# Score attention phase of a gated cross-attention stack: TensorE's order in half 1, the query banks, and two groups of warm-up matmuls

## The reference, cut to what matters

```python
# L1 feed-forward: dense base product plus a sparsely gated low-rank product
logits = sigmoid(xf @ router_W.T)                       # 32 values, each repeated twice
logits = repeat(logits, 2) + biases
top_v, top_i = top_k(logits, 8)
gating = sparse / sum(sparse) * 8
out = xf @ base_W.T + 2.0 * ((xf @ A.T) * gating) @ B.T
# L2 "score" attention: queries and keys come from the context, the layernorm of x
# multiplies the scores elementwise, and the softmax itself is the block's output
scores = (ctx @ Wq.T + bq) @ (ctx @ Wk.T + bk).T / 8 * layernorm(x)
x = x + tanh(g) * softmax(where(mask, -inf, scores))
# L2 experts: their router
logits = layernorm(x) @ router_w.T                      # 8 experts, top 2, capacity 64
```

## Time and profile before

| | |
|---|---|
| median of three runs | 1154.47 us (1151.9 to 1156.37) |
| the profiled execution's own time | 1155.46 us |
| its span, first to last instruction | 1153.7 us |
| mean granted TensorE clock | 0.939 of full speed |
| TensorE busy | 1016.7 us, 88% of the span |
| VectorE, ScalarE, GpSimd busy | 708.8, 483.2, 195.4 us |

### The profile page before, as it was taken

One profiled execution on the slowest core, in us unless ns is written; L12 is line 12 of the kernel. 1 busy time (PEld: TensorE's weight loads), 2 busy tenths in 40 slices (PEclk: granted clock), 3 DMA queues, 4 the chain that ended last, 5 costly groups with the idle time before them and its releaser, 6 DMA issues. The chain is left out here.

```text
span 1153.7 us, 23269 instructions
## 1 busy us (share of the span) xinstructions
PE 1016.7 (88%) x9296; PEld 830.5 (72%) x9296; DVE 708.8 (61%) x1737; ACT 483.2 (42%) x863; POOL 195.4 (17%) x167
## 2 busy tenths in 40 slices
PE   7979889769998899999789999885796989889997
PEld 4747777658777687878678887674694777677886
DVE  0667768766776665564576666666535677654544
ACT  1447767613343335444233333334442334333443
POOL 4100000020001133444430000032101000133342
PEclk8999999988999899999899999986797999888999
DMA  8600000000001122333000000010100000122232
GB/s 291 226 2 3 2 1 2 2 1 1 2 3 34 52 94 77 99 96 97 8 1 2 2 2 2 1 38 1 37 1 1 2 3 18 33 96 80 87 106 69
DMA packets 17707, 48.29 MB, mean 42 GB/s; under 512 B 3072, under 2 KB 5248, under 8 KB 17472
## 3 DMA queue, kind: packets, MB, share of 16 engines
q1 hardware_dynamic: 17600, 46.80, 12.5%
HBM read 45.61 MB, written 1.05 MB: 40 GB/s over the span
## 5 line engine op out<-in xcount | busy, mean ns | idle before, releaser
L1567 POOL TENSOR_TENSOR p_WML<-p_raw,p_WMH 128x768 fp32r<-128x768 f32 x56 | 103.5, 1849 | 173.8 <-ACT p_WMH L1652 168.3
L1683 ACT ACTIVATE p_AHI<-p_A 128x512 fp32r<-128x512 f32 x62 | 39.2, 632 | 168.5 <-DVE p_A L1765 168.5
L1765 DVE TENSOR_TENSOR p_A<-p_A,PS 128x512 f32<-128x512 f32 x62 | 42.6, 688 | 85.0 <-PE PS L1615 84.4
L1288 ACT ACTIVATE p_E<-PS 128x768 f32<-128x768 f32 x64 | 51.6, 807 | 83.3 <-PE PS L1139 83.3
L1393 DVE TENSOR_REDUCE p_mx<-PS 128x2 f32<-128x512 f32 x64 | 44.1, 689 | 59.2 <-PE PS L1103 59.1
L737 PE MATMUL PS<-p_FT,p_PTS 128*128 128x128 f32 x512 | 65.2, 281 | 16.1 <-DVE XNS L889 14.8
L737 PEld LDWEIGHTS PS<-p_FT,p_PTS 128*128 128x128 f32 x512 | 61.2, 195 | 22.0 <-DVE p_PTS L925 20.7
L1769 DVE TENSOR_TENSOR p_ALO<-p_A,p_AHI 128x512 fp32r<-128x512 f32 x62 | 44.8, 723 | 43.2 <-ACT p_AHI L1683 43.2
L83 PE MATMUL PS<-p_WMH,p_AHI 128*128 128x256 f32 x224 | 63.1, 282 | 3.5 <-DVE p_ALO L1769 3.3
L85 PE MATMUL PS<-p_WMH,p_ALO 128*128 128x256 f32 x224 | 62.5, 279 | 0.0
L84 PE MATMUL PS<-p_WML,p_AHI 128*128 128x256 f32 x224 | 62.5, 279 | 0.0
(11 more groups left out here) (504 smaller groups left out, 3290.7 us busy)
## 6 DMA issues: line engine op xcount, KB each, us to landing
p_raw<-in_moe SPq DMA_DIRECT2D x56, 448.0 KB, 3.3
p_fr<-in_fold SPq DMA_DIRECT2D x16, 480.0 KB, 4.5
p_raw<-in_wpack SPq DMA_DIRECT2D x8, 416.0 KB, 6.2
p_early_raw<-in_moe SPq DMA_DIRECT2D x6, 448.0 KB, 3.2
CP<-in_consts SPq DMA_DIRECT2D x1, 1725.0 KB, 9.9
XS<-in_x SPq DMA_DIRECT2D x1, 1024.0 KB, 14.9
W2R<-in_ffn SPq DMA_DIRECT2D x4, 256.0 KB, 3.6
p_W3R<-in_ffn SPq DMA_DIRECT2D x4, 256.0 KB
```

What stands on the lines that cost most here:

```text
L1288: act.activation(E[:, n % 4], PS[:, ST:ST + 2, 0:384], ACT.Exp, scale=scale).then_inc(s["ex"], 1)
L1567: g.tensor_tensor(WML[:, n % RING, :], raw[:, i % RAW, 0:SEL], WMH[:, n % RING, 0:SEL].bitcast(F32), ALU.subtract).then_inc(s["w_lo"], 1)
L1765: v.tensor_tensor(A[:, b, :], A[:, b, :], PS[:, GS_BANK, :], ALU.mult).then_inc(s["ag"], 1)
```

## The change

TensorE's list is changed in one place: `base(1)` moves from behind `query_keys(1)` to directly behind `mid_router(1)`, ahead of `lora(0)`; `lora_turned(1)` moves ahead of the wait for both evictions and asks for one of them only; the queries and keys of half 1 go to banks 3 and 7 in place of 0 and 1. Two groups of eight warm-up matmuls are added, one behind `transposes(0)` and one behind `transposes(1)`. The lists of the other engines stay as they are.

```diff
--- before.py
+++ after.py
@@ -2182,7 +2182,7 @@
                 CNT = ph.sb("CNT", [P, NT, 2 * NE])
                 junk = ph.sb("junk", [P, 1])
 
-                QP, TR, BASE, MR, MT, SC = (((7, 3), (0, 1)), (0, 0), (4, 0), (2, 6), (7, 3), (6, 2))
+                QP, TR, BASE, MR, MT, SC = (((7, 3), (3, 7)), (0, 0), (4, 0), (2, 6), (7, 3), (6, 2))
 
                 with nc.Block() as block:
                     @block.sync
@@ -2241,7 +2241,7 @@
                         def lora_turned(h):
                             for t in range(TT):
                                 pe.wait_ge(s[h]["ga"], t + 1)
-                                pe.wait_ge(s[0]["q_raw"], 2)
+                                pe.wait_ge(s[h]["q_raw"], 2 if h == 0 else 1)
                                 m = pe.transpose(PS[0:LR, MT[h], t * P:t * P + P], M[h][:, t, :], ident)
                             m.then_inc(s[h]["mt"], 1)
 
@@ -2277,11 +2277,12 @@
                         lora_turned(0)
                         pe.wait_ge(s[1]["t1_lo"], KC)
                         mid_router(1)
+                        base(1)
                         lora(0)
+                        pe.wait_ge(s[0]["q_raw"], 2)
                         query_keys(1)
+                        lora_turned(1)
                         pe.wait_ge(s[1]["q_raw"], 2)
-                        base(1)
-                        lora_turned(1)
                         scores(0)
                         lora(1)
                         scores(1)
@@ -2289,7 +2290,9 @@
                         pe.wait_ge(s[1]["es"], 2)
                         warm(pe, WARM["mid"], bank=BASE[0])
                         transposes(0, s[0]["n3"], s[0]["t3_done"], BASE[0])
+                        warm(pe, WARM["split"], bank=3)
                         transposes(1, s[1]["n3"], s[1]["t3_done"], BASE[1], s[1]["n3d"])
+                        warm(pe, WARM["split"], bank=3)
                         for h in range(HALVES):
                             logits(h)
                         for h in range(HALVES):
```

## The result

The changed kernel took 1159.36 us in the median of eight runs (1156.88 to 1161.44), the kernel before 1154.43 us in eight of its own (1151.9 to 1156.64). The ratio is 1.0036, 95% interval 1.0018 to 1.0053: about 4 us slower. The profiled execution took 1157.01 us, only 1.55 above the profiled one of before; its phases ahead of the changed one, whose code is the same, happened to be 1.8 us shorter.

A forecast was written before the change was run, and what follows sets the result against it. No engine fills the phase; a chain passing from engine to engine bounds it. 1155.46 + 2.7 - 1.0 = 1157.2 us for an execution like the profiled one, 0.99 above the median, so forecast 1156.2 us; range 1152.6 to 1159.6.

The forecast's parts named there:

- rival (b): Second warm-ups ahead of the logits warm nothing, logits stay at 0.213 us each: +4.5, 1159.0 us; chance 0.08.
- The queue on GpSimd: Queries 1 finish late behind base(1), delaying GpSimd's list, its statistics and half 0's normalisation and scores: +2.7 us.
- Its lower bound: In the front, the clock rises one stretch earlier, base(1) ends at 766.9, and the cost is only 1.1 us.
- TensorE's removed wait: TensorE's 0.78 us of waiting for the eviction of queries goes; nobody profits.
- VectorE's wait for the turned middle: VectorE's 2.80 us wait at 773.77, which lora_turned(1) causes, ends in slack; VectorE gains nothing there.
- First warm-ups: Eight behind transposes(0), 1.8 us at full clock, fit the 2.33 us idle ahead of transposes(1): zero cost.
- Second: Warm-ups ahead of the logits cost 1.8 us but speed the logits to 0.104 us each: net gain 1.0 us.
- The rule on weight loads: At the logits, a 128-column weight load takes 107 ns whatever the clock, so a higher clock would gain nothing.
- that moment moves against the rise of the clock: The next phase's start shifts against the clock's rise: put at zero, with 0.7 us either way.
- (a): Clock up earlier or unseen slack in the chain: +1.1 in front, -1.4 behind, 1154.2 us; chance 0.22.
- (d): Another wait hides the front, only the tail counts, next phase starts near a rise: -2.1, 1152.4 us; chance 0.08.
- (c): Clock stays at 1.2 GHz through the changed phase because of added idle time: +9.8, 1164.3 us; chance 0.05.

The follow-up runs named there:

- order: The changed kernel without the two groups of warm-ups, so the new order on TensorE alone; +0.22% (0.04 to 0.40) against the kernel before.
- after_early: The changed kernel with GpSimd's four low parts of weight tiles moved between its low parts of queries 0 and 1; +0.03% (-0.17 to 0.23) against the kernel before.
- warm: The kernel before, old order on TensorE, with only the two groups of warm-ups added; +0.03% (-0.17 to 0.23) against the kernel before.
- after_idle: The changed kernel with six unread additions on VectorE, 2.07 us of idle time, in the changed phase; +0.50% (0.28 to 0.72) against the kernel before.
- after_capidle: The changed kernel with three unread additions on GpSimd, 1.95 us of idle time, right before the last attention phase; +0.30% (0.11 to 0.49) against the kernel before.
- before_early: The kernel before with only GpSimd's weight low parts moved between its low parts of queries 0 and 1; +0.03% (-0.17 to 0.23) against the kernel before.
- warm_early5: warm_early with five in place of eight warm-ups in the second group; 1152.07 us against 1155.65 of the kernel before, -0.30% (-0.48 to -0.13).
- warm_early: The kernel before with both warm-up groups and GpSimd's weight low parts moved between low parts of queries 0 and 1; +0.11% (-0.12 to 0.35) against it.

## Why the prediction was right, and which term was missed

- **The number** was right in part by luck. The range reached up to 1159.6 us because it took in rival (b) at 1159.0, whose mechanism the runs rule out (below); the forecast was 1156.2, and the bounds of the sum itself, 2.7 - 0.8 = 1.9 with 0.7 us of clock, end at 1157.1. What held are the steps inside the changed phase.
- **The queue on GpSimd** was right in mechanism and size: 2.7 us worked out, 2.9 measured at the normalisation; `base(1)` itself took 5.3 us, from 761.35 to 766.67, where 5.1 were worked out. Its lower bound (given as 1.1, by its own terms 1.3; clock up one stretch earlier) was met in `order` with 1.4. That the cause is GpSimd's list and not the wait itself is shown by `after_early`: the same order on TensorE, with that list rearranged, makes the phase 3.6 us shorter.
- **TensorE's removed wait** was worth nothing, as said. VectorE's wait for the turned middle stayed.
- **First warm-ups: nothing**, as said. **Second: a gain**, sized at 1.0 with bounds 0.8 to 1.4; 1.5 in the changed kernel and in `warm`. The clock held through all 48 logits there, which is the outer bound. In `after_idle` and `after_capidle`, the same code up to there, it fell as half 1's were about to start, which is the inner one, and the gain was less than that bound: the normalisation came 2.9 us later than before and half 1's routing 2.3, a gain of 0.6. So the changed phase costs 1.4 us in two of its four profiles and 2.3 in the other two.
- **The rule on weight loads** of the Trainium skill ("TensorE: Matmul & The Clock Gate", section "LDWEIGHTS (loading the stationary operand)"), by which the logits would keep their pace: the trace contradicts it for the low clock. The same matmuls took 0.213 us each at 0.50 and 0.108 at 1.00, and `after_idle` and `after_capidle` have both levels in one execution, with half 1's 24 at 0.213. Rival (b), which has the nearest number, is out.
- **What failed** is the sentence "that moment moves against the rise of the clock; I put it at zero, with 0.7 us either way". It was written of the next phase's start and is about right for it (53.3 us both times). But it was applied to one phase only. The last attention phase, one further on, stood in the kernel before where the clock rises earliest of all fourteen profiles, so a shift could hardly gain there and cost +1.9 and +2.6 us in the two profiles of the changed kernel. With it the sum would have been 3.3 to 4.1 us, against +4.1 (2.1 to 6.1) and +2.4 (0.1 to 4.8) measured.
- **Rivals**: (a), a shorter front, and (d), a hidden one, fell with the profile of the changed kernel; the clock rise of (a) did occur in `order`. (c), slower by a clock that stays low through the phase, didn't happen there; that the slow clock would be found two phases later was in none of them.

## What to carry to other kernels

When a step moves on one engine, follow its consumers into the lists of the other engines: here 2.9 us of a block of matmuls of 5.3 us reached ScalarE's normalisation through GpSimd's list, in which 5 us of weight work that nothing in front waited for stood ahead of the statistics. And where a program is a chain of phases with idle gaps, don't stop at the end of the phase: compare every later phase's length and the clock at its start, and take a measured change of a few microseconds for the sum of both. A phase's gain can be given back whole by a shift (`before_early`), and kept by another that ends 0.2 us away from it (`warm_early5`); a gain of that kind may not outlive the next edit.

## What the runs showed that I had not expected

- Moving a phase by 1 to 3 us changed the length of an untouched one by 1.9 to 2.8 us, in two groups (142.3 to 142.8, 144.2 to 145.1).
- The clock's first rise lay 5.0 to 5.3 us into the changed phase in all fourteen profiles, although that phase began between 745.8 and 754.4 us.
- A VectorE operation on 128x4 elements took 1.10 and 1.19 us beside a running GpSimd instruction, 0.17 otherwise.
- Single executions of one kernel spread over up to 13 us (`warm_early`, 1151.8 to 1164.8), several times the effects studied, so the time of one profiled execution ranks no two of these kernels. Lengths of single phases repeat better, though not always: the third phase, which no kernel here changes, took 156.6 to 162.1 us, and the changed one 68.7 us twice and 69.6 once for the same code.
